# Reordering the cross steps of a two-layer decoder, and pairing transposed scores with projections in its self steps

## The reference, cut to what matters

```python
x = x + attn(ln(x), ...)            # layer 0: window of +-32 positions, 16 heads of 16
x = x + xattn(ctx, ctx, ln(x), pad) # layer 0: cross attention to 77 context rows, padded
x = x + moe(ln(x), ...)             # layer 0: 8 experts, top 2
x = x + attn(ln(x), ...)            # layer 1: causal
x = x + xattn(ln(x), ctx, ctx, mask)# layer 1: cross attention, mask of 256 x 77
x = x + ffn(ln(x), ...)             # layer 1: quantised feed-forward

def attention(q_in, kv_in):         # each of the four, per batch item
    q, k, v = q_in @ Wq + bq, kv_in @ Wk + bk, kv_in @ Wv + bv
    p = softmax(q @ k.T / 4 + mask) # 16 heads
    return (p @ v) @ Wo + bo
```

## Time and profile before

| | us |
|---|---|
| median of 3 runs | 2263.77 (2261.82 to 2269.98) |
| the profiled execution | 2267.25 |
| its span | 2265.6 |
| mean granted clock of TensorE | 0.947 of full |

### The profile page before, as it was taken

One profiled execution on the slowest core, in us unless ns is written; L12 is line 12 of the kernel. 1 busy time (PEld: TensorE's weight loads), 2 busy tenths in 40 slices (PEclk: granted clock), 3 DMA queues, 4 the chain that ended last, 5 costly groups with the idle time before them and its releaser, 6 DMA issues. The chain is left out here.

```text
span 2265.6 us, 57078 instructions
## 1 busy us (share of the span) xinstructions
PE 2012.9 (89%) x19754; PEld 1641.0 (72%) x19754; DVE 1269.4 (56%) x5456; ACT 983.6 (43%) x1905; POOL 688.6 (30%) x1244
## 2 busy tenths in 40 slices
PE   7999987778886999999999789989888788899889
PEld 5788876667665999999999577777666666444367
DVE  5788875554542111011105688888666765549974
ACT  2555554554441333333333255555544444247510
POOL 3666653244453000000001545543312221003410
PEclk9999999898977999999999899999988989999999
DMA  6333332222326999999995543343222222000023
GB/s 209 113 112 111 114 108 81 74 81 85 97 70 235 407 344 346 339 339 342 343 340 207 175 134 123 119 132 114 74 82 76 86 77 66 5 0 1 0 56 93
DMA packets 209554, 334.73 MB, mean 148 GB/s; under 512 B 59501, under 2 KB 193426, under 8 KB 200306
## 3 DMA queue, kind: packets, MB, share of 16 engines
q1 hardware_dynamic: 194914, 301.82, 38.8%
q0 software_dynamic: 9552, 26.10, 3.8%
q10 hardware_dynamic: 4928, 4.72, 0.6%
HBM read 193.74 MB, written 28.05 MB: 98 GB/s over the span
## 5 line engine op out<-in xcount | busy, mean ns | idle before, releaser
L2205 ACT ACTIVATE moe_h<-moe_h_ps,moe_weights 128x128 f32<-128x128 f32 x424 | 132.8, 364 | 255.2 <-PE moe_h_ps L2173 226.0
L1335 ACT ACTIVATE causal_prob<-causal_ps 128x768 f32<-128x768 f32 (+1 forms) x192 | 169.0, 880 | 161.8 <-PE causal_ps L1640 160.2
L2638 PE MATMUL ffn_prod_ps<-x_sb,ffn_weights 128*128 128x512 f32 x480 | 209.8, 596 | 7.0 <-ACT ffn_sig_q L2624 7.0
L2237 DVE TENSOR_TENSOR moe_y<-moe_y_ps,moe_weights 128x256 f32<-128x256 f32 x53 | 22.5, 425 | 328.1 <-PE moe_y_ps L2185 328.1
L2173 PE MATMUL moe_h_ps<-moe_h,moe_weights 128*128 128x128 f32 x1696 | 198.0, 275 | 0.0
L2173 PEld LDWEIGHTS moe_h_ps<-moe_h,moe_weights 128*128 128x128 f32 x1696 | 193.6, 192 | 0.1
L2116 POOL DMA_DIRECT2D moe_y_dram<-moe_y x71 | 39.5, 557 | 492.4 <-DVE moe_y L2237 484.2
L2638 PEld LDWEIGHTS ffn_prod_ps<-x_sb,ffn_weights 128*128 128x128 f32 x480 | 90.6, 191 | 123.9 <-issue 109.6
L1028 DVE CUSTOM_DVE_ANT_0 causal_masked<-causal_ps,causal_causal_mask 128x256 bf16<-128x256 f32 (+1 forms) x512 | 152.0, 352 | 37.4 <-PE causal_ps L1606 37.2
L1028 DVE CUSTOM_DVE_ANT_0 window_masked<-window_ps,window_window_mask 128x160 bf16<-128x160 f32 x512 | 135.0, 319 | 44.2 <-PE window_ps L1606 42.9
L1606 PE MATMUL causal_ps<-k_pair,q_pair 64*128 64x78 f32 (+2 forms) x1024 | 107.5, 310 | 26.6 <-DVE causal_m_tok L1028 19.3
(11 more groups left out here) (411 smaller groups left out, 5001.4 us busy)
## 6 DMA issues: line engine op xcount, KB each, us to landing
moe_weights<-moe_w_in SPq DMA_DIRECT2D x53, 2180.0 KB, 9.7
q_pair<-parts SPq DMA_DIRECT2D x512, 128.0 KB
parts<-moe_w_in SPq DMA_DIRECT2D x17, 2180.0 KB, 8.9
k_pair<-parts SPq DMA_DIRECT2D x256, 128.0 KB
k_pair<-parts SPq DMA_DIRECT2D x256, 38.5 KB
moe_y_dram<-moe_y POOLq DMA_DIRECT2D x71, 128.0 KB, 3.9
moe_rows<-moe_slots_dram SPq DMA_DIRECT2D x53, 128.0 KB, 3.5
x_before_ffn_dram<-x_sb SPq DMA_DIRECT2D x16, 256.0 KB, 2.1
```

The costliest lines, as they stand in the source:

```text
L1335: nc.scalar.activation(out, src, ACT.Exp).then_inc(expd, 1)
L2205: nc.scalar.activation(out[:, f, :], psum[:, f // 2, (f % 2) * TM:(f % 2) * TM + TM], ACT.Gelu, bias=bias[:, f:f + 1]).then_inc(done, 1)
L2638: op = nc.tensor.matmul(prod_ps[:, slot, f, :].rearrange("p (b t) -> p b t", b=2), w[:, k, at:at + P], x_cols(n // GROUPS, k), start=(k == ...
```

## The change

Cross steps get a new order on all engines; k is stacked before q for the first half; k's parts for the next item are made one step ahead; the output projection moves to the other PSUM tile. In self steps each pair of transposed score matmuls is followed by one K chunk of the phase 0 projection of that slot. Cut to its core:

```diff
+        def out_ps(ref):
+            return psa if wide(ref) else psb
 # SP
+                        first_k = layer_at(ref).cross and hf == 0
+                            if first_k: wait k_lo, k_hi   # else q_lo, q_hi
                         ... wait s2_mm as before
+                        if first_k:
+                            stack_k(par, hf, pairs, nk)
+                            sp.wait_ge(q_lo, t + 1); sp.wait_ge(q_hi, t + 1)
+                        stack_q(par, hf, pairs)
                         ... k second otherwise; the tail's store moves behind the stacks
 # POOL
+                        if i == 0 and wide(ref) and active(ref, -1):
+                            context(t + 1, ref + 1)
+                            layernorm(t + 1, ref + 1)          # was slot 3
+                        if i == 3 and wide(ref) and active(ref, 1):
+                            place_values(t - 1, ref - 1)       # was the end of the step before
+                        if i == 3 and wide(ref):
+                            padding(t, ref)
                         if i == 3 and inline(ref - 1, 7) and inline(ref, 7):
-                            scatter(t - 1, ref - 1, range(ST, ST * 2))
+                            if wide(ref) and ref < N:
+                                pool.wait_ge(stacks_begun, t)
+                            scatter(t - 1, ref - 1, range(0 if wide(ref) and ref < N else ST, ST * 2))
 # DVE
-                    if active(ref, 2):
+                    if active(ref, 2) and not (wide(ref - 1) and wide(ref)):
                         split_max(t, ref, 2, 1)                # now slot 6 of the step before
+                        if i == 4 and wide(ref):
+                            next_rows(t, ref)                  # was slot 7
-                        if i == 1 and active(ref, 4):
+                        if i == (4 if wide(ref) else 1) and active(ref, 4):
                             add_output(t, ref, 4)
-                        if i == 2 and in_tail(ref, 4):
+                        if i == (6 if wide(ref) else 2) and in_tail(ref, 4):
                             ... statistics of the next layer norm
+                        if i == 1 and tail and in_tail(ref - 1, 4) and wide(ref):
+                            tail_rows(t - 1, ref - 1)          # was slot 7 of the step before
+                        if i == 6 and wide(ref) and wide(ref + 1) and active(ref, 1):
+                            split_max(t, ref, 1, 1)
-                        if i == 4 and active(ref, 0):
+                        if i == 4 and active(ref, 0) and not wide(ref):
+                            low_key(t, ref)
+                        if i == 6 and wide(ref + 1) and active(ref, -1):
+                            low_key(t + 1, ref + 1)
 # ACT, a cross step: keep_xT, exponentials 0, apply_norm of the step before, max_rows(2, 1),
 # query_high, see, exponentials 2, keep_heads(3, 1), exponentials 4, next_key_high, keep_values,
 # max_rows(1, 0), keep_turned, exponentials 6, keep_heads(2, 0), keep_oT
+                def next_key_high(t, ref):
+                    for hf in range(2):
+                        act.wait_ge(stacked[hf], t * 16 * STACK_DMAS)
+                    key_high(t + 1, ref + 1)
 # PE
-                    for j in range(L.pairs):
-                        for kt, q0, nq, col in L.shifted:
+                    for j in range(L.pairs):
+                        for n, (kt, q0, nq, col) in enumerate(L.shifted):
                             for ab in range(2): ... matmul
-                    op.then_inc(s2_mm, 1)
+                            if j == L.pairs - 1 and n == last:
+                                op.then_inc(s2_mm, 1)
+                            if beside is not None:
+                                beside(n)
+                def beside(t, ref, i, now, ks):       # ks: one of the two K chunks
+                    if i == 0 and active(ref, 4):
+                        output(t, ref, 0, ks)
+                    if i == 2 and now:
+                        query(t, ref, 0, ks)
+                    if i == 3 and now and not layer_at(ref).cross:
+                        key(t, ref, 0, ks)
+                    if i == 4 and now:
+                        value(t, ref, 0, ks)
+                def wide_slot(t, ref, i, now):
+                    # 0 scores, turn_normed, shifted     1 query 0, late_maxima
+                    # 2 scores, query 1, shifted, route_products, last_quads
+                    # 4 scores, shifted, output 0, value 0   5 output 1, value 1
+                    # 6 scores, early_maxima, heads_out, last_turn, shifted
+                    # 7 first_quads, turn_outputs
```

More of the change, by code:

```diff
@@ L1446, in step @@
                     now, shift = active(ref, 0), active(ref, 2)
[L1448 removed]
+                    if now:
                         keep_xT(t)
@@ new lines, in narrow_slot @@
+                def narrow_slot(t, ref, i, now):
+                    if active(ref, 1):
+                        scores(t, ref, i)
+                    if i == 0 and now:
+                        turn_normed(t, ref)
+                    if i == 1 and active(ref, 4):
+                        output(t, ref, 1)
+                    if i == 3 and active(ref, 2):
+                        late_maxima(t, ref)
+                    if i == 3 and now:
+                        query(t, ref, 1)
+                    if i == 4 and now and not layer_at(ref).cross:
+                        key(t, ref, 1)
+                    if i == 4 and in_tail(ref, 5):
+                        last_turn(t, ref)
+                    if i == 5 and now:
+                        value(t, ref, 1)
+                    if i == 6 and active(ref, 3):
+                        heads_out(t, ref)
+                    paired = active(ref, 2)
+                    if paired:
+                        shifted(t, ref, i, lambda k: beside(t, ref, i, now, (k,)))
+                    elif i != 1:
+                        beside(t, ref, i, now, range(KC))
+                    if i == 1 and ref == 0:
+                        pe.wait_ge(scaled[0], 1)
+                    if i == 1 and active(ref, 3):
+                        last_quads(t, ref)
+                    if i == 2 and (inline(ref, 6) or inline(ref, 7)):
+                        route_products(t, ref, inline(ref, 6), inline(ref, 7))
+                    if i == 3 and ref == 0:
+                        pe.wait_ge(loaded[0], 16 * n_load[0])
+                    if i == 3 and ref == STEPS - 1 and tail:
+                        pe.wait_ge(peak_found, 3)
+                        nc.tensor.transpose(ps2[0:1, 0, 0:P], whole_top[:], ident[:]).then_inc(top_turned, 1)
+                    if i == 6 and active(ref, 1):
+                        early_maxima(t, ref)
+                    if i == 7 and active(ref, 2):
+                        first_quads(t, ref)
+                    if i == 7 and active(ref, 3):
+                        turn_outputs(t, ref)
+                    if i == 7 and emptied(ref) and active(ref, 3):
+                        keep_warm(DRAIN_WARM // 2, ps2)
+                    if i == 7 and (ahead(ref, 6) or ahead(ref, 7)):
+                        route_products(t + 1, ref + 1, ahead(ref, 6), ahead(ref, 7))
@@ L1936, in step @@
-                        if i == 3 and active(ref, 2):
-                            late_maxima(t, ref)
-                        if i == 3 and now:
-                            query(t, ref, 1)
-                        if i == 4 and now and not L.cross:
-                            key(t, ref, 1)
-                        if i == 4 and in_tail(ref, 5):
-                            last_turn(t, ref)
-                        if i == 5 and active(ref, 1) and not narrow:
-                            early_maxima(t, ref)
```

354 lines of the change are left out of this document (201 added, 153 removed).

## The result

The changed kernel takes 2152.31 us (median of four runs, 2144.61 to 2155.14) against 2266.88 (2261.82 to 2270.13): ratio 0.9491, 95% interval 0.9458 to 0.9524. The forecast was 2165 in a range of 2120 to 2215. The profiled execution has a span of 2142.9 us, 122.7 less than before; it is the fastest of the four.

The account below looks back on a forecast made before the run. Self steps were taken as bound by TensorE's work, cross steps by waits and the clock: 93 us from 28 cross steps plus 6 from the last ones, 2267.25 - 99 = 2168, 2165 against the median; range 2120 to 2215.

Parts of the forecast that it names:

- What bounds it, and which waits go: Cross steps: bound by waits and their effect on the clock; waits of 3.03 us a padded, 3.17 a masked step go.
- The clock rises with them: Cross steps: the granted clock goes from 0.89 to full, worth 1.8 us a padded and 1.75 a masked step.
- rival 1: Cross steps: the waits go but the clock stays at 0.89, so 50 us stay; 2190 to 2215, chance 0.15.
- Half of the waits come back: Cross steps: new waits cost half of what was removed, 1.5 us a padded and 1.6 a masked step.
- the named waits: TensorE's waits in the cross steps for stack, low parts, head copy and residual add: 39.4 us padded, 41.2 masked.
- the 14.85 of no return: Masked cross step in us without the removed waits, at the full clock, before any new wait is added.
- the 15.4: Padded cross step in us without the removed waits, at the full clock, before any new wait is added.
- Edits on other engines at nothing: Single edits on POOL, ACT and the tail's store were costed at nothing, ACT's earlier `see` included.
- Rival 4: Cross steps: SP's sixteen issues a step become the bound, half 1 lands late; slower, up to 2320, chance 0.04.
- Self steps at nothing: Self steps: mixing projection with shifted matmuls changes nothing; at best 22 us gained, at worst 52 lost.
- Rivals 2, 3 and 5: VectorE bound in cross steps, 2215, chance 0.1; later self-step exponentials, 2217, 0.05; no change that can be told, about 2260, 0.04.
- The steps outside the stretches: Two last cross steps of each kind, without projections: 1.5 us gained each, 6 us, between 0 and 13.

Follow-up runs that it names:

- The fillers: Extra matmuls nobody reads: eight ahead of padded steps' first scores, kernel before, 2250.99 us; three behind the routing products, changed kernel, 2138.74 us.
- the unmixed kernel: The changed kernel with the self steps' projections back behind the shifted matmuls, as before the change; 2151.50 us, ratio 0.9494.

## Why the prediction was right, point by point

- **What bounds it, and which waits go.** Right. The stack, the low parts, the head copy and the add in front of `query` are gone. The runs bear out two of the causes: undoing the early keys brings waits for the stack and for k's low part back, undoing the late value its own. The wait that the earlier exponentials brought, 14.3 us for the copy of the row maxima, was none of those that I had named. That the head copy and the add in front of `query` went by their own edits no run tested.
- **The clock rises with them.** Right in the main. I took 1.8 and 1.75 us a step, 46 us over the 26 steps of the two stretches; busy time fell by 44.5, of which some 7 by the estimate above is not clock. It is split otherwise: 1.25 a padded step and 2.2 a masked one, since the routing products kept one fall of the clock in most padded steps, part of rival 1. The fillers bear on that clock by itself: 15 us of the padded stretch in the kernel before, 9 in the changed one.
- **Half of the waits come back.** This term was mis-sized. I took 1.5 and 1.6 us a step, 40 us of 81 over the same steps. The idle time fell by 74.1, so 6.5 came back net, 0.25 a step. That is two things. Waits do stand at the places that I named (`last_quads` behind `seen`, `first_quads` behind the copy, `early_maxima` behind the add): 8.9, 4.0 and 4.9 us, 17.8 together, each 0.4 to 0.5 long. But my sum had also left standing 20.4 us of idle time that were not among the named waits (50.9 less 39.4, and 50.1 less 41.2), and these had places in the old order that the new one doesn't have. The largest in the padded steps, of `late_maxima`:

```profile
PE window_psa L1749 <- issue: 7.6, 13, 0.8
```

Masked steps came out at 14.76, the 14.85 of no return; padded ones before the routing below the 15.4.
- **Edits on other engines at nothing.** Nothing in the changed kernel's time speaks against it: VectorE, ScalarE and GpSimd are no bound. But the reason was too weak. I treated ScalarE's order and VectorE's rows as neutral details; each is a condition of the gain, 88 and 64 us.
- **SyncE.** The four issues for the queries of half 0 take 2.49 us again and are out five microseconds ahead. Half 1 starts at 491.03, is issued by 496.3 and lands some 2 us later, 5.6 us into a step whose scores begin at 492.7; I had 4.9. Rival 4 is out as a bound, though its sign, scores that wait for a k stack, shows in three masked steps with 2.2 us in all.
- **Self steps at nothing.** Right, and shown by the unmixed kernel.
- **Rivals 2, 3 and 5** are out: TensorE's waits name no row maxima in the cross steps, and the longest of the casts in the masked ones takes 0.72 us where it took 1.99, ScalarE's later exponentials do not show in the self steps, and the time moved by 5%.
- **The steps outside the stretches.** I gave 6 us for the last two of each kind and 6.65 for the fourteenth that takes an item in; all that lies outside the two stretches gained 4.1. The fourteenth steps did more than their part: from their first shifted scores to the next step's they went from 21.4 to 15.4 us and from 19.5 to 13.8. But the steps behind them, the first of each last two, got longer, from 13.9 to 17.0 and from 14.2 to 15.0, so for these the forecast had the wrong sign; what their new order costs no run asked. And the third and fourth causal steps are the long ones in this execution, 3.6 us more together than before.

The sum in one line: 86.5 us were forecast for these 26 steps and 118.6 came; of the 32.1 us between them the returning waits make 33.8, and the busy time takes 1.6 back. With 8.4 less than forecast outside, 122.7 came between the profiled executions where 99 were forecast. That 2165 lies only 12.7 us from 2152 is in part luck: the profiled execution before stood 3.5 us above its median, and the one after stands 7.7 below.

Open: what makes two routing steps of nine keep their clock in the same order; and whether GpSimd's new order and the other PSUM tile for the output are needed, which no run tried in the changed kernel by itself.

## What to carry to other kernels

Where engines hand work round in a circle, an order is one object. Price a reordering by what each new neighbour waits for, and test it by taking single parts out, not by adding them: VectorE's early rows are worth 64 us inside the new order and, with GpSimd's norm, cost 15 in the old one. A microsecond of new wait on TensorE cost 2.1 us here where its clock fell with it (0.93 to 0.84), and 1.2 where the clock stayed at 0.97 or above; so price waits with the clock taken in. And look at what stands right before each stretch at the lower clock: one short idle time there went with 1.6 us a step, and moving the products one group ahead removed both.

## What the hardware showed that I had not expected

Useless matmuls can pay: 27.7 us of them made a stretch of 263.0 us 15.3 shorter, as the granted clock rose from 0.89 to 0.96. And a pause of 0.49 us behind matmuls of 8 and 16 columns was followed by some 3 us at 0.50 in seven of nine steps, while a pause of 0.44 to 0.54 us behind shifted scores of 256 columns, once in each of the same steps, was not. Which difference between the two places matters no run shows. The latter in the changed kernel's timeline, TensorE's shifted scores and `first_quads`:

```profile
490.57 0.43 PE L1721 MATMUL window_ps<-q_pair,k_pair 64*77 64x256 f32 x4
491.44 1.07 PE L1744 MATMUL window_psa<-window_prob,v_aug 77*32 77x256 f32 x16 [0.44 <-issue]
```
